# First attention layer of a four-layer graph network: a PSUM copy of the softmax exponentials as VectorE's second operand

## What is computed

```python
q = (x @ Wq + bq).reshape(n, 8, 32)
k = (x @ Wk + bk).reshape(n, 8, 32)
v = (x @ Wv + bv).reshape(n, 8, 32)
time_diff = edge_time - node_time[dst]
time_features = stack([sign(time_diff), log1p(abs(time_diff) / 3600.0)], axis=-1)
scores = einsum('ehd,ehd->eh', q[dst], k[src]) * scale + time_features @ Wt + bt
alpha = softmax(scores, axis=0)
msg = alpha[..., None] * v[src]
out = segment_sum(msg, dst, num_segments=n).reshape(n, 256) @ Wo + bo
x = layernorm(x + out)
```

## Time and profile before

| | us |
|---|---|
| median of 3 runs | 9408.56 |
| lowest and highest run | 9382.79, 9411.95 |
| span of the profiled execution | 9608.8 |
| first to last multiplication L1276 / L1283 of the first attention layer, about | 1228 to 4250 |

### The profile page before, as it was taken

The page is one execution under the profiler, slowest core; times in us unless marked ns, Lnnn a source line. Parts: engine busy times, 40 slices in busy tenths (PEclk is TensorE's granted clock), DMA queues, the critical chain, the costliest instruction groups (busy, mean ns, idle before and its releaser), DMA issues. The chain is left out here.

```text
span 9608.8 us, 121761 instructions
## 1 busy us (share of the span) xinstructions
PE 6035.1 (63%) x27004; PEld 3698.3 (38%) x27227; DVE 5624.6 (59%) x14481; ACT 2416.0 (25%) x7255; POOL 5956.5 (62%) x5564
## 2 busy tenths in 40 slices
PE   2121155555555555547999997899999997554544
PEld 0010033333333333334444444555555555333333
DVE  4100055555555555556888887899999998222224
ACT  0000033333333333322333332344444443000000
POOL 5777655555555555546888884566666665666663
PEclk6555566666666666668999998999999999667676
DMA  1000032223222232322332333344444444333334
GB/s 64 1 10 10 17 88 83 83 78 83 81 80 80 81 83 78 81 55 73 85 84 85 84 84 52 111 120 119 119 119 121 120 119 101 90 90 89 89 90 55
DMA packets 405871, 777.59 MB, mean 81 GB/s; under 512 B 195938, under 2 KB 225356, under 8 KB 405196
## 3 DMA queue, kind: packets, MB, share of 16 engines
q0 software_dynamic: 279488, 712.60, 28.4%
q1 hardware_dynamic: 126348, 64.59, 2.3%
HBM read 736.75 MB, written 40.07 MB: 81 GB/s over the span
## 5 line engine op out<-in xcount | busy, mean ns | idle before, releaser
L495 POOL DMA_INDIRECT rec_s<-wts,rows x784 | 780.5, 995 | 1085.2 <-ACT rows L467 870.5
L1829 POOL DMA_INDIRECT gat<-y,rec_sb_s x892 | 1182.5, 1326 | 298.0 <-issue 278.8
L2098 POOL DMA_INDIRECT gat<-x,rec_sb_d x892 | 846.5, 949 | 484.5 <-issue 266.2
L965 POOL DMA_INDIRECT gat<-kv,rec_sb_d x896 | 906.7, 1012 | 334.7 <-issue 272.9
L1381 POOL DMA_INDIRECT gat<-kv,rec_sb_s x900 | 861.5, 957 | 398.5 <-issue 313.9
L2113 PE MATMUL ps<-gat,oh 128*128 128x256 f32 x1760 | 648.5, 538 | 680.2 <-DVE acc L2133 253.6
L1577 DVE TENSOR_REDUCE small<-ps 128x2 f32<-128x1024 f32 x884 | 1041.7, 1216 | 6.9 <-PE ps L1445 5.7
L434 POOL DMA_INDIRECT rec_d<-small x784 | 810.7, 1034 | 343.0 <-issue 265.1
L1870 PE MATMUL ps<-big,oh 128*128 128x512 f32 x1760 | 947.3, 637 | 0.0
L2113 PEld LDWEIGHTS ps<-gat,oh 128*128 128x128 f32 x1760 | 462.9, 274 | 865.5 <-issue 497.1
L1048 PE MATMUL ps<-big,oh 128*128 128x264 f32 x1768 | 754.1, 541 | 0.3
(11 more groups left out here) (276 smaller groups left out, 13129.7 us busy)
## 6 DMA issues: line engine op xcount, KB each, us to landing
gat<-kv,rec_sb_s POOLq DMA_INDIRECT x900
gat<-kv,rec_sb_d POOLq DMA_INDIRECT x896
rec_sb_s<-rec_s SPq DMA_DIRECT2D x448, 32.0 KB, 2.2
gat<-y,rec_sb_s POOLq DMA_INDIRECT x892
gat<-x,rec_sb_d POOLq DMA_INDIRECT x892
rec_d<-small POOLq DMA_INDIRECT x784
rec_s<-wts,rows POOLq DMA_INDIRECT x784
rec_s<-gat SPq DMA_DIRECT2D x4, 1808.0 KB, 16.7
```

The source lines that it names most:

```text
L495: e.indirect_dma_start(out=recs["s"], out_offset=bass.IndirectOffsetOnAxis(ap=pr[:, t:t + 1], axis=0), in_=rr[:, t, :], in_offset=None).th ...
L965: e.indirect_dma_start(out=gat[:, m.u, q, :], out_offset=None, in_=table, in_offset=bass.IndirectOffsetOnAxis(ap=r_sb[:, m.u, q, 0:1].bitc ...
L1829: e.indirect_dma_start(out=rows_y[m.u][:, q, :], out_offset=None, in_=y1, in_offset=bass.IndirectOffsetOnAxis(ap=r_sb[:, m.u, q, 0:1].bitc ...
L2098: e.indirect_dma_start(out=gat[:, m.u, q, 0:D], out_offset=None, in_=x3, in_offset=bass.IndirectOffsetOnAxis(ap=r_sb[:, m.u, q, 0:1].bitca ...
```

## The change

In the first attention layer ScalarE takes the exponentials twice: once into `pvb` as before, and once into 32 columns of the PSUM bank that the macro's sums will use (columns 264 to 295 of bank 5 or 6). The semaphore `p` is stepped by the second. VectorE's multiplication reads its second input from that copy, stretched over 32 columns. Before both, ScalarE waits for one more semaphore: that the sums of the macro two before have been added (`flush`), since they lie in the same bank.

```diff
@@ attention
             psO = [ps[:, 5 + v if timed else 3, 0:AC] for v in range(2)]
+            psP = [ps[:, 5 + v, AC:AC + Q * H] for v in range(2)]
@@ act
                 e.wait_ge(s["f"], m.done())
                 e.wait_ge(s["sum"], m.done(2))
+                e.wait_ge(s["flush"], m.done(2))
                 A.activation(pvb[:, m.v, :, :].rearrange("p q (h c) -> p q h c", c=HC)[:, :, :, DH],
-                             v4(sm), ACT.Exp).then_inc(s["p"], 1)
+                             v4(sm), ACT.Exp)
+                A.activation(psP[m.v], sm, ACT.Exp).then_inc(s["p"], 1)
                 A.activation(ff[m.v], dd, ACT.Exp).then_inc(s["ef"], 1)
@@ weight_values
-                engine.tensor_tensor(pw[:, :, :, 0:DH], gv, pw[:, :, :, DH:HC].to_broadcast([P, Q, H, DH]),
+                engine.tensor_tensor(pw[:, :, :, 0:DH], gv, bcast(v4(psP[m.v]), 3, [P, Q, H, DH]),
                                 ALU.mult).then_inc(s["pv"], 1)
```

## The result

The changed kernel took 9580.45 us (median of 4 runs, 9568.78 to 9584.24), the kernel before 9409.03 us beside it (9382.79 to 9411.95). The ratio is 1.0184, with an interval of 1.0161 to 1.0207: 171 us or 1.8% slower. The forecast was slower by 98 us; the direction was right, and the time lies 30 us above the range. (In a later group of runs one of the 19 runs of the kernel before took 17330.32 us beside 9641.84 to 9683.02 us for the others, and no ratio counts it.)

The account below looks back on a forecast made before the run. No engine was full; a ring of waits bound the first attention loop: POOL's issues, the gather burst's end, DVE's and ACT's tail. Longer passes 86 + activation 12 = 98 us, 9408.56 + 98 = 9507 us, 1.0% slower; range 9374 to 9550.

Parts of the forecast that it names:

- The stretch: POOL's gather issues in the first attention loop, lengthened beside the two-SBUF-input multiplication; mean should fall from 1013 to 960 ns.
- The second rival: No change: gather issues stay long or hardly matter, leaving only ACT's cost, 9421 us, or about 9380 to 9400; chance 0.23.
- Shorter issues make longer passes: POOL's passes in the first attention loop: without long gather issues all become long ones, costing 86 us over 111 passes.
- The first rival: Faster: each pass of the loop shortens by what POOL saves, -47 + 12 = -35 us, 9374 us; chance 0.20.
- its own test: Faster case decided by POOL's wait at the end of an unstretched pass: it holds if that falls below about 8.8 us.
- the 47 us: POOL's issue time in the loop, removed when gathers are no longer held up: (1013 - 960) ns x 884.
- 52 of 106 passes grow by 1.58 us: POOL's stretched passes, mean 26.66 us, become 28.24 us like the unstretched: 82 us, or 86 us for the loop's 111.
- carried over unchanged: The 200 us between the profiled span and the median of the runs, kept as an offset: 9706.8 becomes 9507 us.
- ACT's 12 us: Added activation on the pass's tail, ahead of the ring fill: 0.11 us x 111 passes, bounds 0 and 28 us.
- The hole in the burst: A delayed third gather opens a gap in the first gather burst; PE's results get through; 0.7 us saves 2.2 us.
- the end of the burst: PE results not handed over before a gather burst are handed over when it ends; DVE, ACT, ring fill and POOL follow.

Follow-up runs that it names:

- operand_only: Kernel before, with only the multiplication's second input moved to PSUM, holding ones instead of exponentials: 8328.81 us, ratio 0.9804.
- compact_sbuf: Changed kernel with the second set of exponentials in 32 adjoining SBUF columns instead of PSUM: 9629.96 us, ratio 1.0049 against the kernel before.
- operand_d: Kernel before, with only the multiplication's second input moved to PSUM, holding ones, where before took 9664.84 us: 9771.78 us, ratio 1.0112.
- hold_d: Changed kernel plus a 704-column memset on POOL ahead of each macro's third gather, where before took 9664.84 us: 9689.77 us, ratio 1.0028.
- change_d: The changed kernel run again, where the kernel before took 9664.84 us: 9763.58 us, ratio 1.0106.
- before_d: The kernel before, unchanged, profiled again where it took 9664.84 us: 9658.33 us, ratio 0.9995.
- act_only: Kernel before plus only ScalarE's part (second exponentials into PSUM, wait for flush), multiplication still reading SBUF: 8497.46 us, ratio 1.0003.
- half_after: Changed kernel gathering only the keys' half of each row in the first layer: 9699.96 us, ratio 1.012 against the kernel before.
- woven: Changed kernel with POOL's gathers and scatters interleaved so no four gathers come in a row: 9711.07 us, ratio 1.0133 against the kernel before.
- again: The kernel before, unchanged, run again for an ordinary profile: 8498.38 us against 8495.57 us, ratio 1.0004.

## Why the prediction was right or wrong

**The stretch: right.** L965's mean fell to 959 ns, no gather was long, and the product with its second operand in PSUM kept its duration. Reading both inputs from SBUF is the cause, not the broadcast or the layout: operand_only removes the stretch (mean 964 ns), compact_sbuf keeps it (996 ns, 23 gathers over 1.5 us). The second rival (the stretch stays) is refuted. The Trainium skill ("SBUF — State Buffer", Who interferes with whom) has `tensor_tensor` not stall descriptor generation; the traces disagree, with issues of 1.78 us beside 0.98 us, and 172 us of POOL's time in them on an early chip. Which part of an indirect DMA's issue is held up, the reading of its row numbers from SBUF or the making of descriptors, no run separates.

**Shorter issues make longer passes: right in direction where PE's results come late.** operand_d shows the one way (issues shorter, loop 77 us longer), hold_d the other (158 us of memset, loop 57 us shorter than change_d's). The first rival ("POOL's saving counts") failed in the first comparison, and by its own test: single waits are at 9.2 us. But it is what happens on the early chips, where POOL waits 2.1 us for L467 instead of 870.5: 2% faster. Its price, 35 us, came from the 47 us of a late chip's profile; where POOL never waits, 195 issues are stretched beside 221 products, and the stretch is worth 172 us.

**The term that failed: "52 of 106 passes grow by 1.58 us", and with it "carried over unchanged".** The sum was made on one execution 200 us above the median, and I took the other executions to have the same share of short passes, with the 200 us as an offset. On the late chip, where the profiled before_d (9656.43 us) is an ordinary run, the working nearly holds: sorted as in the prediction its 52 passes with a stretch of 0.5 us or more have a mean of 26.96 us, the 48 without it or another pause 28.37, so the sum is 52 x 1.41 = 73 us, 77 us for 111 passes, and 89 us with ACT's 12. The loop grew by 92 us and the time by 99. In the first comparison it did not hold: 171 us, of which the loop took only 67 against the profile shown. What an ordinary execution of before did there was never profiled. If its untouched parts took what they took in the profile after, 6478 us, its loop had 9407 - 6478 = 2929 us, which is 2929 / 111 = 26.4 us per pass: nearly all passes short, against 27.84 after. For it speaks that the profile shown looks like one of the late chip outside the loop too: 1210 us up to the first gather where the late chip's profiles have 1209 to 1215 and the kernel after 1181, and 2032 us for the second attention's gathers where they have 2013 to 2051 and the kernel after 1959. It stays an inference from two spans, and no run settles it: the runs at 9409 us may as well have had the loop of 3022 us and other parts some 90 us shorter than in the kernel after. So it is shown that the count of short passes times 1.58 us, with the offset carried over, does not give the 171 us; where the missing 73 us come from stays open. If the inference holds, it would make the count of passes that had a short form to lose about twice what I took (111 in place of 52). The prediction considered the opposite only, that runs without a profile might already consist of long passes.

**ACT's 12 us: not confirmed.** The step is 0.12 us as taken. On an early chip it costs nothing that shows (act_only, 1.0003). On the late chip operand_d, without it, took 8 us more than change_d as a whole (9771.78 and 9763.58 us) and 15 us less in the loop (3125.2 and 3139.9 us), so the runs allow nothing as well as 12 us. That the forecast's 98 us and the late chip's 99 us agree so exactly is partly luck: the forecast was made for another comparison, and the sum from before_d gives 89.

**The hole in the burst: wrong as a mechanism.** The prediction said that a late third gather leaves a hole in the transfers, in which PE's results get through. half_after has such holes in every burst and woven has no burst of four, and both stay at 1.012 and 1.013. The prediction also had the end of the burst hand over the results; in half_after the transfers end 0.9 us earlier and the release does not. What goes with a shorter pass, in all but one of the short passes on the late chip and in the first comparison, is a stretch of time inside the pass in which POOL begins no new indirect DMA: an issue of over 1.3 us, another pause, a memset. It is not enough by itself, as counted above. Why a step of PE's semaphore is handed over late while POOL issues, on some chips and not on others, stays open. So does why a delay of 0.7 us can win more than its own length: where results come late, the passes under 27.5 us have a mean of 26.1 to 27.0 us in each kernel, the others one of 28.1 to 28.5 us.

**No version beats both kernels everywhere.** On the early chips the changed kernel is the fastest of all that ran (8319.5 us). On the late chip the kernel before is, with the changed kernel and memset 0.28% behind it; the order of the two turns with the chip.

## What to carry to other kernels

A VectorE product of two SBUF operands next to indirect DMAs issued by GpSimd cost GpSimd 0.78 us per product where GpSimd never waited (172 us for 221 products), and up to 1.05 us for one (an issue of 2012 ns beside 960). Moving one operand to PSUM removed it, for one activation that takes a step of 0.12 us. It paid only where GpSimd's issuing was the bound, so look first at whether that engine waits at the end of its pass. And before a sum is made on a profiled execution that lies 2% above the median, ask which of its terms the ordinary execution shares: a count of short and long passes need not carry over as an offset does.

## What the runs showed of the hardware

- One program, unchanged, took 8491 to 8496 us on two chips and 9586 to 9665 us on a third, with the first comparison at 9409 us. In the slower places PE's results are handed over late: of DVE's wait before L1216, 610.4 us end "remote" in before_d, and on an early chip (again) the whole wait is 3.0 us. The granted TensorE clock differs as well (mean 0.788 in before_d, 0.818 in again), yet PE is not busy for longer in the slower place, but for 60 us less in the loop:

```profile
1211.00:4290.00 3079.00, 1601.12 (x6018) 1053.42 (x6018) 1624.86 (x6005) 951.60 (x2679) 1687.05 (x1679) 0.68 0.30 81
```
```profile
1104.00:3428.00 2324.00, 1660.74 (x6018) 1073.08 (x6018) 1594.24 (x6003) 951.46 (x2674) 1810.83 (x1679) 0.72 0.40 107
```

  (columns as in the earlier trace rows; before_d and again). The engines do the same work in 3079 and in 2324 us, and none is busy for longer by more than 31 us in the slower place; the difference is waiting.
- The sign of the change goes with that: 0.98 on the early chips, 1.011 and 1.018 where results come late.
- A load added to an engine can make the program faster: 158 us of memset on POOL made the changed kernel 74 us faster on the late chip (9763.58 to 9689.77 us), and the kernel before still was 25 to 31 us faster than that.
